# Centring h in place on GpSimd for the covariance, and moving copies on ScalarE, in a two-layer convolution kernel

## The chip, the core and the metric

The program runs on one core of a Trainium2 chip. The metric is the device time of one execution, in microseconds (us). The core's engines are TensorE (PE in the profile, its weight loads PEld), VectorE (DVE), ScalarE (ACT), GpSimd (POOL) and SyncE (SP), which issues most DMAs. Each engine works through its own list of instructions in order and waits on semaphores for the others.

## What is computed

Layer 0 makes position-dependent 7x7 filters from x and applies them. Layer 1 is a bottleneck block with batch normalisation over the batch; its second half is where the change lies. Cut to that:

```python
x = _L0_conv_ref(x, ...)                                  # (4, 256, 64, 64)
h = relu(_bn_train(_conv(x, w1, 1, 0), g1, b1))           # 64 channels
h = relu(_bn_train(_conv(h, w2, 1, 1), g2, b2))           # 64 channels, 3x3
h = _bn_train(_conv(h, w3, 1, 0), g3, b3)                 # 256 channels, 1x1
return relu(h + residual)                                 # residual is layer 1's x
```

`_bn_train` subtracts the mean of each channel over batch and pixels and divides by the root of its variance plus 1e-5.

## The kernel before

Most of the 822 us is layer 0 (to about 670 us). After it come the 3x3 convolution (680 to 740 us), whose result lies in `y`, eight images of 128 partitions x 1024 (two rows' halves of 64 channels share the partitions), then three short stages that this document is about.

**Batch norm 2 and ReLU (742 to 760 us).** VectorE works out `scale` and `shift` from statistics; ScalarE applies them with ReLU in place, image by image (`relu(i, ...)`, line 1274, semaphore `relu2`), and also sums each image. The first image goes in two halves.

**Covariance (745 to 767 us).** The variance after the last 1x1 convolution is not measured on its 256 channels. It is worked out from the 64x64 covariance of h and the weights. For that h is needed with pixels on the partitions, so 16 blocks of 512 columns go through a loop of three engines:

- `hT_of(k)` on TensorE transposes four 128-column tiles of block k (image k//2) into one of four PSUM banks, `hT_bank(k)`. Ahead of it `centre(k)` (line 1687) fills the bank with minus a per-channel constant c, the larger of 0 and batch norm 2's offset, and the transposes add to it.
- The block is split in a high part (fp32r) and a low part, the rest: a cast by VectorE (line 2181) or, for blocks 11, 13 and 15 (`UPPER_BY_ACT`), a copy by ScalarE (`upper(k)`), and then a subtraction by VectorE (`hT_parts`, line 1760). Both go to `hT[:, k % 2]`, so block k may be written once `gram(k-2)` is done.
- `gram(k)` (line 1712) multiplies the parts on TensorE. TensorE's list is transposes of k, product k-2, transposes of k+1, and so on; the first four blocks have no bank to wait for.

**Batch norm 3 (767 to 771.6 us).** A chain between VectorE and TensorE (`link` makes each operation wait for the one before) ends in `affine(2, 2, ...)`, which gives `scale` and `shift` of the last layer; ScalarE takes a root in between.

**Last layer (770 to 817 us).** The 1x1 convolution is 32 products m of 1024 columns (`last(m)`), each of two times three matmuls on the high and low parts of h (`h2_hi`, `h2_lo`; `h_hi` and `h_lo` in the profile) and of the weights. VectorE scales a product and adds the residual (line 2302, `f_added`), ScalarE adds `shift` and applies ReLU (line 1311, `f_out`), SP stores 1 MB after every second one (line 576). Product m waits for `f_added` of m-4, since there are four pairs of banks.

The parts of h come from two lists that fill gaps: ScalarE copies the high part of an image (`h2_high(i)`, line 957) right behind the ReLU of the next image, and GpSimd subtracts it from `y` (line 951, `h2_lo_done`). The outputs of unit 0 overwrite `y[:, 4:8]`, so ScalarE's first output waits for six low parts and its third for eight. A load of the residual into `y[:, 0:4]` waits for four.

Quoted, since the order within it matters:

```python
link(dve.tensor_tensor(gm[:, 10:12], gm[:, 4:8:2], gm[:, 4:8:2], ALU.mult))      # L2290
link(dve.tensor_tensor(mv[:, 12:12 + width], mv[:, 2:2 + width], gamma, ALU.mult))  # L2187
dve.tensor_tensor(scale[:, i:i + width], mv[:, 10:10 + width], gamma, ALU.mult)     # L2190
dve.scalar_tensor_tensor(out=shift[:, i + j:i + j + 1], in0=mv[:, 10 + j:11 + j], scalar=mv[:, 12 + j:13 + j],
                         in1=beta[:, j:j + 1], op0=ALU.mult, op1=ALU.add)           # L2192, twice
```

## Time and profile before

| | us |
|---|---|
| median of 3 runs (822.2 to 824.45) | 822.55 |
| the profiled execution | 823.44 |
| its span, first to last instruction | 821.6 |
| its granted TensorE clock, mean | 0.993 |

| engine | busy us (share of the span) |
|---|---|
| PE | 781.9 (95%) |
| DVE | 659.2 (80%) |
| ACT | 382.0 (46%) |
| POOL | 350.3 (43%) |

The span leaves out 1.8 us of the execution (823.44 less 821.6). Starts are counted from the span's first instruction. A row of a timeline joins neighbours of one form (x4), and "idle before" names what ended an engine's idle time. Shares over the whole span say little on the three short stages, which are read by themselves below.

### The profile page before, as it was taken

The numbers are of one execution on the slowest core, as the hardware profiler recorded it, in microseconds if no ns is written. First come the engines' busy times: TensorE is split into PE (matmuls) and PEld (weight loads), VectorE is DVE, ScalarE is ACT, GpSimd is POOL, SyncE is SP. The second block draws the span as 40 slices with busy tenths as digits, with TensorE's granted clock in tenths as the row PEclk, the third lists the DMA queues.
The fourth block names the chain that finished last, engine by engine and source line by source line (L and its number), as shares of the span: only waits on it lengthen the run. The fifth ranks groups of instructions, "written<-read, shape, count | busy, mean of one in ns | idle before, by whom it ended". The sixth has DMA issues, their size and how long they took to land.

```text
span 821.6 us, 13801 instructions
## 1 busy us (share of the span) xinstructions
PE 781.9 (95%) x4973; PEld 715.1 (87%) x4973; DVE 659.2 (80%) x908; ACT 382.0 (46%) x663; POOL 350.3 (43%) x253
## 2 busy tenths in 40 slices
PE   6799989999999999999999999999998998999996
PEld 2259988899999999999999999999997886777785
DVE  4989798897699588868977995888648676978896
ACT  3542222444344434434433434344326777727586
POOL 4345663484268238524852682385220012515300
PEclk9899999999999999999999999999999999999998
DMA  9932235957994899499588948885887869805598
GB/s 271 374 137 53 52 80 158 234 153 202 179 243 117 237 177 243 114 242 193 151 211 173 246 116 236 154 211 126 208 154 232 267 196 307 321 1 196 202 376 353
DMA packets 250108, 162.17 MB, mean 197 GB/s; under 512 B 191881, under 2 KB 232826, under 8 KB 247226
## 3 DMA queue, kind: packets, MB, share of 16 engines
q1 hardware_dynamic: 241322, 141.83, 66.4%
q10 hardware_dynamic: 8720, 19.47, 7.3%
q8 instruction: 41, 0.67, 0.4%
q14 instruction: 25, 0.20, 0.1%
HBM read 99.48 MB, written 56.36 MB: 190 GB/s over the span
## 4 chain that ended last, share of the span: by engine, by line
PE 78%; DVE 9%; issue 4%; DMA 3%; ACT 3%; POOL 1%; SPq 1%; DVEq 0%; ACTq 0%; POOLq 0%
PE ps L1319 21%; PE ps L1321 21%; PE ps L1320 21%; PE ps L1439 4%; PE ps L1455 3%; PE ps L1489 3%; DVE logit L1941 1%; DMA b2raw<-in_L_conv_b 1%; PE ps L1712 1%; DMA bands<-wide 1%; DVE whole L1851 1%; PE ps L1331 1%; DVE wpart L1801 1%; POOL ring L875 1%; PE ps L1704 1%
## 5 line engine op out<-in xcount | busy, mean ns | idle before, releaser
L875 POOL TENSOR_TENSOR ring<-whole,ring 128x576 fp32r<-128x576 f32 x112 | 194.9, 1746 | 281.3 <-ACT ring L957 281.3
L1319 PE MATMUL ps<-w_hi,ring 128*128 128x336 f32 x832 | 275.5, 331 | 6.7 <-POOL ring L875 3.8
L1321 PE MATMUL ps<-w_hi,ring 128*128 128x336 f32 x832 | 262.7, 316 | 0.0
L1320 PE MATMUL ps<-w_lo,ring 128*128 128x336 f32 x832 | 261.4, 314 | 0.0
L1319 PEld LDWEIGHTS ps<-w_hi,ring 128*128 128x128 f32 x832 | 157.3, 189 | 16.9 <-issue 10.6
L1320 PEld LDWEIGHTS ps<-w_lo,ring 128*128 128x128 f32 x832 | 157.3, 189 | 0.0
L1321 PEld LDWEIGHTS ps<-w_hi,ring 128*128 128x128 f32 x832 | 156.4, 188 | 0.0
L957 ACT ACTIVATE ring<-whole 128x576 fp32r<-128x576 f32 x112 | 87.1, 781 | 91.9 <-POOL whole L870 53.1
L957 ACT ACTIVATE band_hi<-ps 128x320 fp32r<-128x320 f32 (+1 forms) x128 | 53.1, 419 | 127.5 <-PE ps L1439 119.9
L1319 PE MATMUL ps<-band_hi,xT_hi 128*128 128x224 f32 (+2 forms) x320 | 94.6, 296 | 1.6 <-DVE xT_lo L1760 1.2
L1321 PE MATMUL ps<-band_hi,xT_lo 128*128 128x224 f32 (+2 forms) x320 | 92.3, 288 | 0.0
L1320 PE MATMUL ps<-band_lo,xT_hi 128*128 128x224 f32 (+2 forms) x320 | 92.3, 288 | 0.0
L1851 DVE SCALAR_TENSOR_TENSOR whole<-xbuf 128x576 f32<-128x576 f32 x80 | 81.0, 1018 | 8.5 <-POOL ring L875 8.3
L1760 DVE TENSOR_TENSOR band_lo<-ps,band_hi 128x320 fp32r<-128x320 f32 (+1 forms) x128 | 57.9, 457 | 24.9 <-ACT band_hi L957 24.0
L957 ACT ACTIVATE xT_hi<-ps 128x512 fp32r<-128x512 f32 x64 | 37.9, 596 | 74.1 <-PE ps L1455 72.3
L886 POOL TENSOR_TENSOR xbuf<-xbuf 128x1152 f32<-128x1152 f32 x24 | 65.2, 2719 | 0.9
L1319 PEld LDWEIGHTS ps<-band_hi,xT_hi 128*128 128x128 f32 x320 | 60.7, 190 | 3.8 <-issue 1.8
L1760 DVE TENSOR_TENSOR xT_lo<-ps,xT_hi 128x512 fp32r<-128x512 f32 x64 | 43.6, 684 | 25.1 <-ACT xT_hi L957 25.1
L1941 DVE SCALAR_TENSOR_TENSOR logit<-ps,logit 128x480 f32<-128x480 f32 x80 | 52.3, 653 | 13.5 <-PE ps L1321 9.6
L1439 PE MATMUL ps<-ident,raw 128*128 128x128 f32 x352 | 60.6, 276 | 2.1 <-DVE band_lo L1760 1.7
L1320 PEld LDWEIGHTS ps<-band_lo,xT_hi 128*128 128x128 f32 x320 | 60.7, 190 | 1.0
L1321 PEld LDWEIGHTS ps<-band_hi,xT_lo 128*128 128x128 f32 x320 | 60.9, 190 | 0.0
(228 smaller groups left out, 1353.5 us busy)
## 6 DMA issues: line engine op xcount, KB each, us to landing
xq<-in_x SPq DMA_DIRECT2D x108, 256.0 KB, 4.7
raw<-bands SPq DMA_DIRECT2D x32, 768.0 KB, 7.1
xbuf<-in_x SPq DMA_DIRECT2D x16, 1024.0 KB, 8.9
x_dram<-x ACTq DMA_DIRECT2D x31, 512.0 KB, 5.2
bands<-wide SPq DMA_DIRECT2D x64, 199.0 KB, 5.0
x1in<-x_dram SPq DMA_DIRECT2D x6, 2048.0 KB, 20.4
out<-x1in SPq DMA_DIRECT2D x12, 1024.0 KB, 3.9
bands<-wide SPq DMA_DIRECT2D x3, 1792.0 KB, 15.9
```

Of the source, the lines that this page charges most:

```text
L875: pool.tensor_tensor(split(k, 1), positions(whole[:, k % TBUFS, :], 0, 2), split(k, 0).bitcast(F32), ALU.subtract).then_inc(sig_lo_done, 1)
L886: pool.tensor_tensor(a, b, a, ALU.subtract).then_inc(c_done, 1)
L957: return act.activation(dst, src, ACT.Copy)
L1319: pe.matmul(dst, l_hi, r_hi_, start=first, stop=False, **kw)
L1320: pe.matmul(dst, l_hi, r_lo_, start=False, stop=False, **kw)
L1321: return pe.matmul(dst, l_lo, r_hi_, start=False, stop=last, **kw)
L1439: mm = pe.transpose(bank[:, i * P:(i + 1) * P], src, ident[:, :])
L1455: mm = pe.transpose(bank[:, t * C + kb * P:t * C + (kb + 1) * P], src[:, kb, 4 * t:4 * t + 4, g % 2::2], ident[:, :])
L1489: mm = pe.matmul(bank, v1pack[:, cb, :], r[:, cb, :], start=(cb == 0 and j == 0), stop=(cb == CB - 1 and j == 1))
L1760: return dve.tensor_tensor(dst, a, b, ALU.subtract)
L1851: dve.scalar_tensor_tensor(out=dst, in0=a, scalar=factor, in1=b, op0=ALU.mult, op1=ALU.add).then_inc(done, 1)
L1941: dve.scalar_tensor_tensor(out=dst, in0=m, scalar=factor, in1=src, op0=ALU.mult, op1=ALU.add).then_inc(comb_done, 1)
```

## The change

Instead of adding -c in PSUM by a product for each block, GpSimd subtracts c from h in place in `y` after the ReLU (nine `tensor_scalar`, one for each half of image 0 and one for each further image, semaphore `centred`). The transposes and the high parts wait for `centred` in place of `relu2`. The low parts stay on GpSimd, behind the nine. Since h is then centred in the last layer too, its mean and the covariance's mean are the same vector, and one column of the mean product goes. ScalarE takes the high parts of seven blocks instead of three, and its high parts of h stand behind them. Of the warming products after the 3x3 convolution there are 12 instead of 5.

```diff
-        UPPER_BY_ACT = (11, 13, 15)
+        UPPER_BY_ACT = (3, 5, 7, 9, 11, 13, 15)
...
             pool.memset(cov[:, :], 0.0).then_inc(cov_zero, 1)
-            pool.memset(one[:, :].bitcast(F32), 1.0).then_inc(one_made, 1)
...
+            pool.wait_ge(center_done, 3)
+            for i, c0, c1, made in [(0, 0, HALF, 1), (0, HALF, SPX, 2)] + [(i, 0, SPX, i + 2) for i in range(1, 8)]:
+                pool.wait_ge(relu2, made)
+                pool.tensor_scalar(y[:, i, c0:c1], y[:, i, c0:c1], gm[:, 2:3], None, ALU.add).then_inc(centred, 1)
             for i in range(8):
                 pool.wait_ge(h2_hi_done, i + 1)
...
             def h2_high(i):
-                act.wait_ge(relu2, i + 2)
+                act.wait_ge(centred, i + 2)
                 copy(h2_hi[:, i, :], y[:, i, :]).then_inc(h2_hi_done, 1)
...
             for i in range(1, 8):
                 relu(i, 0, SPX, i)
-                if i < 7:
-                    h2_high(i - 1)
-            upper(11)
-            h2_high(6)
+                if i >= 3:
+                    upper(2 * i - 3)
+            h2_high(0)
             upper(13)
-            h2_high(7)
+            h2_high(1)
             upper(15)
+            for i in range(2, 5):
+                h2_high(i)
             act.wait_ge(bn_dve, BN3_ROOT)
             root(mv[:, 8:10], gm[:, 12:14])
+            for i in range(5, 8):
+                h2_high(i)
...
-            for k in range(4):
-                centre(k)
-            warm(5)
+            warm(12)
...
                 if k >= 4:
                     pe.wait_ge(hT_lo_done, k - 3)
-                    centre(k)
-                pe.wait_ge(relu2, i + 2 if k else 1)
+                pe.wait_ge(centred, i + 2 if k else 1)
...
-            dve.tensor_scalar(center[:, :], ident[:, :], gm[:, 2:3], -1.0, ALU.mult, ALU.mult).then_inc(center_done, 1)
-            dve.wait_ge(center_done, 3)
-            dve.tensor_reduce(gm[:, 2:3], center[:, :].bitcast(F32), AX_X, ALU.add).then_inc(center_done, 1)
+            dve.tensor_scalar(gm[:, 2:3], gm[:, 2:3], -1.0, None, ALU.mult).then_inc(center_done, 1)
...
-            link(dve.tensor_scalar(gm[:, 1:2], gm[:, 3:4], 1.0 / (B * H * W), None, ALU.mult))
...
-            link(dve.tensor_copy(gm[:, 4:8], ps[:, 6, 0:4]))
-            link(dve.tensor_tensor(gm[:, 10:12], gm[:, 4:8:2], gm[:, 4:8:2], ALU.mult))
+            link(dve.tensor_copy(gm[:, 4:6], ps[:, 6, 0:2]))
+            link(dve.tensor_tensor(gm[:, 10:12], gm[:, 4:6], gm[:, 4:6], ALU.mult))
```

ScalarE's list from the ReLU of image 6 to the root, before; `hT<-ps` is a block's high part, `h_hi<-y` an image's:

```order
L1274 ACTIVATE y,sums<-y,shift,scale 128x1024
L957 ACTIVATE h_hi<-y 128x1024 [waits relu2]
L1274 ACTIVATE y,sums<-y,shift,scale 128x1024
L957 ACTIVATE hT<-ps 128x4x128 [waits gram_done,hT_ps]
L957 ACTIVATE h_hi<-y 128x1024 [waits relu2]
L957 ACTIVATE hT<-ps 128x4x128 [waits gram_done,hT_ps]
L957 ACTIVATE h_hi<-y 128x1024 [waits relu2]
L957 ACTIVATE hT<-ps 128x4x128 [waits gram_done,hT_ps]
L1188 ACTIVATE mv<-gm,sums 128x2 [waits bn_dve]
```

The same stretch now:

```order
L1275 ACTIVATE y,sums<-y,shift,scale 128x1024
L958 ACTIVATE hT<-ps 128x4x128 [waits gram_done,hT_ps]
L1275 ACTIVATE y,sums<-y,shift,scale 128x1024
L958 ACTIVATE hT<-ps 128x4x128 [waits gram_done,hT_ps]
L958 ACTIVATE h_hi<-y 128x1024 [waits centred]
L958 ACTIVATE hT<-ps 128x4x128 [waits gram_done,hT_ps]
L958 ACTIVATE h_hi<-y 128x1024 [waits centred]
L958 ACTIVATE hT<-ps 128x4x128 [waits gram_done,hT_ps]
L958 ACTIVATE h_hi<-y 128x1024 [waits centred] x3
L1189 ACTIVATE mv<-gm,sums 128x2 [waits bn_dve]
L958 ACTIVATE h_hi<-y 128x1024 [waits centred] x3
```

Before, six of eight high parts of h stood ahead of block 11's part; now all eight stand behind it, and three of them behind the root.

GpSimd's last instructions now; before, the eight `h_lo<-y,h_hi` came right behind the `step_lo` ones:

```order
L941 TENSOR_TENSOR step<-yin 128x1056 [waits step_lo_done,h1_hi_done,relu1]
L944 TENSOR_TENSOR step_lo<-step,step_hi 128x1056 [waits h1_hi_done]
L949 TENSOR_SCALAR y<-y,gm 128x512 [waits relu2,center_done]
L949 TENSOR_SCALAR y<-y,gm 128x512 [waits relu2]
L949 TENSOR_SCALAR y<-y,gm 128x1024 [waits relu2] x7
L952 TENSOR_TENSOR h_lo<-y,h_hi 128x1024 [waits h2_hi_done] x8
```

All eight low parts now stand behind the centring of the last image.

## Rows read from the trace of the kernel before

**Rows 1.** Busy time of each engine in a stretch (start:end, length, busy, clock, DMA):

```profile
740.00:760.00 20.00, 18.89 (x119) 15.07 (x117) 16.70 (x32) 15.99 (x24) 11.74 (x5) 1.00 0.54 201
```

**Rows 2.** Timeline of VectorE in the loop (start us, us, engine, line, operation, names, forms):

```profile
748.68 0.68 DVE L2181 CAST hT<-ps 128x512 fp32r<-128x512 f32 x1
749.40 0.69 DVE L1760 TENSOR_TENSOR hT<-ps,hT 128x512 fp32r<-128x512 f32 x1
750.01 0.68 DVE L2181 CAST hT<-ps 128x512 fp32r<-128x512 f32 x1
...
763.45 0.69 DVE L1760 TENSOR_TENSOR hT<-ps,hT 128x512 fp32r<-128x512 f32 x1 [0.44 <-ACT hT L957]
...
765.77 0.69 DVE L1760 TENSOR_TENSOR hT<-ps,hT 128x512 fp32r<-128x512 f32 x1 [0.30 <-ACT hT L957]
```

**Rows 3.** Timeline of TensorE, loop and first and last products of the last layer:

```profile
761.55 0.60 PE L1704 MATMUL ps<-ident,y 128*128 128x128 f32 x4
761.91 0.72 PE L1712 MATMUL ps<-hT 128*128 128x256 f32 x4
762.46 0.39 PE L1687 MATMUL ps<-center,one 128*128 128x512 f32 x1
...
770.88 0.39 PE L1319 MATMUL ps<-h_hi,v_hi 128*128 128x512 f32 x1
...
813.88 0.39 PE L1321 MATMUL ps<-h_hi,v_lo 128*128 128x512 f32 x1
```

**Rows 4.** Timeline of ScalarE, end of image 1's ReLU, block 11's high part, first outputs:

```profile
747.05 0.19 ACT L1274 ACTIVATION_READ_ACCUMULATOR y<-y,shift,scale 128x1 f32 x1
...
760.26 0.60 ACT L957 ACTIVATE hT<-ps 128x512 fp32r<-128x512 f32 x1
760.75 1.05 ACT L957 ACTIVATE h_hi<-y 128x1024 fp32r<-128x1024 f32 x1
...
773.00 4.83 ACT L1311 ACTIVATE y<-x1in,shift 128x1024 f32<-128x1024 f32 x4 [2.16 <-DVE x1in L2302]
```

**Rows 5.** Groups of GpSimd by form (count, busy us, mean ns, idle before):

```profile
L951 POOL TENSOR_TENSOR h_lo<-y,h_hi 128x1024 fp32r<-128x1024 f32 x8 | 18.9, 2408 | 23.6 <-ACT h_hi L957 23.6
...
L930 POOL MEMSET v_hi<- 128x1024 f32 x1 | 1.0, 960 | 47.8 <-PE ps L1439 47.8
...
L838 POOL TENSOR_SCALAR_AFFINE_SELECT gavg<-gavg 128x128 f32<-128x128 f32 x3 | 0.9, 294 | 0.4
```

**Rows 6.** Timeline of VectorE, then of GpSimd, in layer 0 around 262 us:

```profile
262.41 0.28 DVE L1978 TENSOR_TENSOR me<-smx,inside 128x112 f32<-128x112 f32 x1
262.72 2.77 DVE L1984 TENSOR_TENSOR wide<-probs,me 128x784 f32<-128x784 f32 x1
265.41 1.98 DVE L1851 SCALAR_TENSOR_TENSOR whole<-xbuf 128x576 f32<-128x576 f32 x1
...
260.22 4.43 POOL L886 TENSOR_TENSOR xbuf<-xbuf 128x1152 f32<-128x1152 f32 x2
264.61 2.15 POOL L875 TENSOR_TENSOR ring<-whole,ring 128x576 fp32r<-128x576 f32 x1
```

**Rows 7.** Forms of line 1978 on VectorE (count, ns min/median/max, first and last start):

```profile
L1978 DVE TENSOR_TENSOR me<-smx,inside x8: 274/276/2179, 125.7 to 625.6; 128x112 f32<-128x112 f32 x8
```

**Rows 8.** Timeline of GpSimd and of VectorE around batch norm 3:

```profile
748.26 18.85 POOL L951 TENSOR_TENSOR h_lo<-y,h_hi 128x1024 fp32r<-128x1024 f32 x8 [23.62 <-ACT h_hi L957]
...
769.81 0.16 DVE L2290 TENSOR_TENSOR gm<-gm 128x2 f32<-128x2 f32 x1
...
771.22 0.34 DVE L2192 SCALAR_TENSOR_TENSOR shift<-mv,bn 128x1 f32<-128x1 f32 x2
771.60 4.96 DVE L2302 SCALAR_TENSOR_TENSOR x1in<-ps,scale,x1in 128x1024 f32<-128x1024 f32 x4
```

**Rows 9.** Stretches after the last product (columns as Rows 1):

```profile
816.00:818.00 2.00, 0.00 (x0) 0.00 (x0) 0.00 (x0) 0.84 (x1) 0.00 (x0) 0.87 0.82 336
818.00:820.00 2.00, 0.00 (x0) 0.00 (x0) 0.00 (x0) 0.00 (x0) 0.00 (x0) 0.50 1.07 442
```

More of the change, by code:

```diff
@@ L267, in build @@
         quad = sb(h1s, "quad", [P, C])
-        center = sb(h1s, "center", [P, P], F32R)
-        one = sb(h1s, "one", [P, P], F32R)
-        rest = sb(h1s, "rest", [P, 2 * MID1 * 9 - 2 * C - 3 * P])
+        rest = sb(h1s, "rest", [P, 2 * MID1 * 9 - 2 * C - P])
         v3raw = sb(h1s, "v3raw", [P, CB, 2, MID1])
@@ L325, in build @@
         c2_done, c2_copied, c2_sum, c2_stat = sem("c2_done"), sem("c2_copied"), sem("c2_sum"), sem("c2_stat")
-        vT_done, center_done, cov_zero, one_made = sem("vT_done"), sem("center_done"), sem("cov_zero"), sem("one_made")
+        vT_done, center_done, cov_zero, centred = sem("vT_done"), sem("center_done"), sem("cov_zero"), sem("centred")
         h2_hi_done, upper_act = sem("h2_hi_done"), sem("upper_act")
@@ L2269, in _ @@
             dve.wait_ge(relu2, 9)
-            dve.wait_ge(center_done, 4)
+            dve.wait_ge(center_done, 3)
             link(dve.tensor_reduce(gm[:, 3:4], sums[:, 0:9], AX_X, ALU.add))
@@ L2288, in _ @@
             dve.wait_ge(means_ps, 1)
-            link(dve.tensor_copy(gm[:, 4:8], ps[:, 6, 0:4]))
-            link(dve.tensor_tensor(gm[:, 10:12], gm[:, 4:8:2], gm[:, 4:8:2], ALU.mult))
-            link(dve.tensor_scalar(mv[:, 2:4], gm[:, 5:8:2], -1.0, None, ALU.mult))
+            link(dve.tensor_copy(gm[:, 4:6], ps[:, 6, 0:2]))
+            link(dve.tensor_tensor(gm[:, 10:12], gm[:, 4:6], gm[:, 4:6], ALU.mult))
+            link(dve.tensor_scalar(mv[:, 2:4], gm[:, 4:6], -1.0, None, ALU.mult))
             dve.wait_ge(sums_ps, 1)
```

11 lines of the change are left out of this document (3 added, 8 removed).

## Prediction

> **What bounds the kernel now.** I read the engines' stretches first [rows 1]: in the 20 us that hold batch norm 2 and the covariance loop no engine is full, but TensorE (18.9) and VectorE (16.7) are near it, so the order of steps decides. VectorE's timeline [rows 2] shows why: a block costs a cast and a subtraction, 1.33 us from cast to cast (748.68 to 750.01), with no idle time before them, and the loop ends with the subtraction of block 15 at 766.46. TensorE's timeline [rows 3] shows 0.36 us for four transposes (761.55 to 761.91) and 0.55 for a product (761.91 to 762.46), and then one product after the other in the last layer: 31 of them from 770.88 to 814.27, 1.40 us each. That layer is bound by TensorE, and 7.3 us pass from its last product to the end of the span. So the change can act on two times: when the loop ends, and when VectorE may begin to empty the banks of the last layer (771.60, [rows 8]), since product 4 waits for the first emptying.
>
> **The loop, made shorter.** Twelve centring products go from it; they lay beside VectorE's work, which set the pace, and are worth nothing by themselves. Four of 13 casts on VectorE go, for ScalarE's copies of 0.60 us [rows 4]. A pair of blocks then costs VectorE at least 1.33 + 0.61 = 1.94 us. The wait that comes in its place is a chain over four blocks: subtraction 0.69, product of that block 0.55, transposes 0.36, next product until its end 0.72, ScalarE's copy 0.60, subtraction 0.61, cast 0.72 [rows 2, 3, 4], with 0.2 for handing over 4.45, or 2.23 a pair. The last pair of before took 2.32 (763.45 to 765.77, [rows 2]) with a centring product in it. I take 2.23, with 1.94 and 2.32 as its bounds.
>
> **The centring, added on GpSimd.** No row shows a `tensor_scalar` there. A memset of the same shape, which reads nothing, took 0.96 us, and the subtraction, which reads two operands, 2.41; a select of 128 columns with one operand took 0.294, or 2.35 if it grows with the columns [rows 5]. One operand is half way: 1.7, bounds 0.96 and 2.41. It is on the path once, in filling the loop: image 1's ReLU ends at 747.24 [rows 4], so its transposes begin at 749.1, the product of block 0 stands between, and the cast of block 2 begins at 749.1 + 0.36 + 0.72 + 0.1 = 750.3 where it was 748.68. Seven pairs later, 15.6 us, the loop ends at 765.9 instead of 766.46: 0.55 earlier. The Trainium skill (GPSIMD Engine Reference, Engine selection) calls GpSimd roughly at line rate with one input. No run here shows that; with some 1.1 us for the centring, an estimate from that page, everything below would come 0.6 us earlier.
>
> **The low parts, moved.** This is the term that counts. The first high part of h now stands behind block 11's, which is copied at 750.3 + 5 x 2.23 - 1.3 = 760.1 (five pairs on, less the copy and the subtraction); so the high part of image 0 is ready at 760.6 + 1.05 = 761.7, and GpSimd works from then for 8 x 2.36 = 18.9 us [rows 8], until 780.6. Before, it was done at 767.11, ahead of the last steps of batch norm 3. Now it runs through all of them, without a gap.
>
> What that does is told by [rows 6] and [rows 7]. `me<-smx,inside`, a sum of two operands in SBUF, takes 0.28 us, and once 2.18. At 262.72 line 1984, with two SBUF operands again, began while GpSimd's operation ran (260.22 for 4.43, two of them, to 264.65), and ended at 265.49: it stood still until GpSimd was through. GpSimd's next operation, in its queue since 264.61, ran then, to 266.76; and line 1851, which VectorE had issued at 265.41, before line 1984 was even done, waited it out, to 267.39. So such an operation waits for the end of the one that GpSimd is at, and GpSimd's next goes ahead of VectorE's next. Operations that read one operand from PSUM don't wait: the casts and subtractions of the loop keep their 0.69 us with GpSimd busy from 748.26 on [rows 2, 8].
>
> In batch norm 3 five operations of VectorE read two SBUF operands: L2290, L2187, L2190 and L2192 twice. They took 0.16 us or so because GpSimd had stopped [rows 8]. Now GpSimd's operations end at 761.7 + 2.36 k: 764.1, 766.4, 768.8, 771.1, 773.5, 775.9, 778.2, 780.6. L2290 comes up at 769.81 - 0.55 = 769.3 and is let through at 771.1, L2187 at 773.5, L2190 at 775.9, the two L2192 at 778.2 and 780.6. If another step (L2291) is caught too, the end stays, because GpSimd has nothing left after 780.6. VectorE begins at 780.8 instead of 771.60. The Trainium skill (SBUF — State Buffer, SBUF: two separate sides) says that such a pair takes the shared port as an exclusive lock for the whole instruction, and names no size below which it does not. No row here shows it for one or two columns, which is what these five have.
>
> **From there to the end.** TensorE has three products' lead over product 4, so what counts is product 4: before at 770.88 + 3 x 1.40 = 775.1, now at 780.8 + 1.24 [rows 8] = 782.1, 7.0 later. In between TensorE stands still for over 7 us. After its last product ended at 814.27 its granted clock was 0.87 in the mean from 816 to 818 and 0.50, the 1.2 GHz level, from 818 on [rows 9]. So it should come back at half clock. What that costs no row shows; at half clock a product takes up to 1.4 us more, so none to two and a half products' worth, 0 to 3.4 us; I take 1.7. ScalarE's first outputs wait for six and eight low parts (775.9, 780.6), which is earlier than VectorE now gives them anything, and the stores follow as before. The remaining edits cost nothing: one link of the chain less lies before the last product, the smaller mean product is off the path, the 12 warming products end before the first transposes, and the load into `y[:, 0:4]` comes at 771, with 34 us left.
>
> Sum: +7.0 + 1.7 = 8.7 us. The profiled execution would have a span of 821.6 + 8.7 = 830.3 and take 832.1; it lies 0.9 above the median of 822.55, from which I count: **831.2**. Bounds of the case: 829.4 (no fall of the clock) to 833.0.
>
> **Rivals.**
> 1. *Not slower: tiny operations are not held up.* If operations of one or two columns slip through, batch norm 3 ends 0.55 earlier. Then the outputs are what is late: ScalarE's third waits for the eighth low part, 780.6 instead of some 775.5, and 30 outputs at 1.21 or less ([rows 4], 4.83 for four, paced by VectorE) end at 816.9 or before, as now. The stores then come closer together than DMA moves them: 15 MB from 783 at 2.4 to 2.5 us each (442 GB/s in [rows 9] at the best) and 1.5 for the landing end at 820.5 to 822. So -1.0 to +0.5, say 822.2. For it: no row has so few columns. Against it: the rows with 112, 784 and 576 columns stand still alike, whatever their own work.
> 2. *Some are caught.* If the neighbours L2190 and L2192 pass together, VectorE begins at 776.1, product 4 at 777.4, +2.3: 824.9. If one boundary is saved, 778.5: +4.7 and little of the clock, 827.5.
> 3. *GpSimd's centring at 2.41 us.* Then it paces the loop, the last image is centred at 764.6, the low parts end at 783.5 and the whole comes to 834.
>
> **How the numbers follow.** The forecast 0.56, rival 1 0.18, rival 2 0.19 (0.06 at 825 and 0.13 above), rival 3 0.07. The forecast, rival 2 and the near side of rival 3 make up about 0.8: 824.0 to 833.2. A measurement of this kernel tells a change from none at about 0.3%, 2.5 us. Slower by more: 0.56 + 0.14 of rival 2 + 0.07 = 0.77. Within: 0.05 + 0.15 of rival 1 = 0.20. Faster, if pairs reach 1.94 us and nothing is held: 0.03.
>
> **What would show it.** In the profile of the changed kernel: L949's mean; VectorE's subtractions of odd blocks 2.2 us apart and the last one ending near 766; L2187, L2190 and L2192 (by their names `mv<-mv,bn`, `scale<-mv,bn`, `shift<-mv,bn`) at around 2.3 us each instead of 0.2, each ending just after one of GpSimd's low parts; `x1in<-ps,scale,x1in` beginning near 781; a gap of 7 us on TensorE and a granted clock of 0.5 after it. The forecast is wrong if these steps keep their 0.2 us while GpSimd is busy, or if GpSimd is done before 771.

## The result, and the profile after

The changed kernel takes **833.17 us** in the median (832.59 to 835.63, 4 runs), the kernel before 823.5 (822.2 to 825.26) beside it. The ratio is 1.0122, with a 95% interval of 1.0091 to 1.0152. The forecast was 831.2, in a range of 824.0 to 833.2. So the sign and most of the size came out. The working did not: one term was several microseconds too small, another several too large, and the end is set by a third thing. The profiled execution took 833.44, with a span of 831.6, 10.0 more than before.

GpSimd's timeline and its groups by form in the changed kernel (start, us; in the groups count, busy us, mean ns, idle before). They answer to [rows 5] and [rows 8].

```profile
744.83 23.00 POOL L949 TENSOR_SCALAR y<-y,gm 128x512 f32<-128x512 f32 x9 [20.72 <-ACT y L1275]
767.79 11.69 POOL L952 TENSOR_TENSOR h_lo<-y,h_hi 128x1024 fp32r<-128x1024 f32 x5
781.07 7.16 POOL L952 TENSOR_TENSOR h_lo<-y,h_hi 128x1024 fp32r<-128x1024 f32 x3 [1.58 <-ACT h_hi L958]
...
L949 POOL TENSOR_SCALAR y<-y,gm 128x1024 f32<-128x1024 f32 x7 | 19.8, 2848 | 0.1
L949 POOL TENSOR_SCALAR y<-y,gm 128x512 f32<-128x512 f32 x2 | 3.1, 1567 | 20.7 <-ACT y L1275 20.7
```

The centring takes 2.85 us for an image, not 1.7, more than the subtraction of two operands (2.38). GpSimd stands in it for 23 us without a gap, and the loop ends with it: the last three subtractions of VectorE's odd blocks begin at 765.15, 767.99 and 770.81, 2.8 us apart. The low parts begin at 767.79 and end at 788.23. In between GpSimd stands still once, for 1.58 us, for want of a high part.

VectorE from the last steps of batch norm 3 on, and ScalarE in the same stretch and at its first outputs (before: [rows 8] and [rows 4]):

```profile
775.20 0.16 DVE L2280 COPY gm<-ps 128x2 f32<-128x2 f32 x1
775.39 1.78 DVE L2281 TENSOR_TENSOR gm<-gm 128x2 f32<-128x2 f32 x1
777.20 2.31 DVE L2282 TENSOR_SCALAR mv<-gm 128x2 f32<-128x2 f32 x1
779.54 0.16 DVE L2284 TENSOR_TENSOR gm<-ps,gm 128x2 f32<-128x2 f32 x1
...
780.80 2.48 DVE L2293 SCALAR_TENSOR_TENSOR x1in<-ps,scale,x1in 128x1024 f32<-128x1024 f32 x2
...
779.74 0.30 ACT L1189 ACTIVATE mv<-gm,sums 128x2 f32<-128x2 f32 x1 [6.22 <-DVE gm L2284]
779.94 2.94 ACT L958 ACTIVATE h_hi<-y 128x1024 fp32r<-128x1024 f32 x3
783.65 2.38 ACT L1315 ACTIVATE y<-x1in,shift 128x1024 f32<-128x1024 f32 x2 [0.77 <-POOL h_lo L952]
788.26 2.34 ACT L1315 ACTIVATE y<-x1in,shift 128x1024 f32<-128x1024 f32 x2 [2.23 <-POOL h_lo L952]
```

Two operations are held up (lines 2281 and 2282), not five. The copy ahead of them reads PSUM and takes 0.16 us with GpSimd busy. Then comes the gap in GpSimd's row: the sixth high part stands on ScalarE behind the root (line 1189), and the root waits for line 2284. So GpSimd has nothing to do until batch norm 3 is nearly through, and VectorE's last five steps meet nobody. VectorE begins to empty the banks at 780.80, which is the prediction's time, for other reasons. ScalarE's third output then waits for the eighth low part until 788.26.

TensorE (first row: transposes waiting for GpSimd) and its stretches (start:end, length, PE busy, clock, DMA share, GB/s):

```profile
750.82 1.12 PE L1699 MATMUL ps<-ident,y 128*128 128x128 f32 x4 [2.17 <-POOL y L949]
...
749.00:756.00 7.00, 5.18 (x24) 0.51 0.24 96
760.00:773.00 13.00, 9.62 (x74) 1.00 0.01 1
773.00:780.00 7.00, 6.52 (x18) 0.51 0.23 74
...
790.00:820.00 30.00, 30.00 (x130) 1.00 0.97 400
```

The granted clock was at its half level, 1.2 GHz, twice, each time after TensorE had stood idle for part of the stretch before (it was busy for 2.3 of the 5 us from 744 to 749, and for 9.62 of the 13 from 760 to 773). From 790 on DMA is busy for 0.97 of the time at 400 GB/s. In the kernel before it still had room (0.91 and 378 GB/s from 780 to 800).

### The profile page after: what moved, and what is told of

Read it like the earlier page. It is cut to its first block, busy times and chain, and to the rows that moved or that the text cites. A ratio compares the mean times of both kernels' runs of the same rounds, so it can differ in the third digit from the quotient of the medians.

```text
span 831.6 us, 13805 instructions
## 1 busy us (share of the span) xinstructions
PE 784.7 (94%) x4964; PEld 719.3 (86%) x4964; DVE 658.2 (79%) x902; ACT 383.0 (46%) x667; POOL 370.2 (45%) x261
## 4 chain that ended last, share of the span: by engine, by line
PE 76%; DVE 10%; issue 4%; POOL 4%; ACT 3%; DMA 1%; SPq 0%; DVEq 0%; ACTq 0%; POOLq 0%
PE ps L1323 21%; PE ps L1325 21%; PE ps L1324 21%; PE ps L1443 4%; PE ps L1459 3%; PE ps L1493 3%; POOL y L949 2%; DVE whole L1845 1%; DVE logit L1935 1%; DMA b2raw<-in_L_conv_b 1%; DVE wsum L1795 1%; DVE wpart L1795 1%; POOL ring L873 1%; POOL whole L868 1%; ACT yin L1205 1%
## 5 line engine op out<-in xcount | busy, mean ns | idle before, releaser
L873 POOL TENSOR_TENSOR ring<-whole,ring 128x576 fp32r<-128x576 f32 x112 | 192.5, 1724 | 283.2 <-ACT ring L958 283.2
L958 ACT ACTIVATE ring<-whole 128x576 fp32r<-128x576 f32 x112 | 87.3, 783 | 92.3 <-POOL whole L868 49.9
L1845 DVE SCALAR_TENSOR_TENSOR whole<-xbuf 128x576 f32<-128x576 f32 x80 | 77.3, 972 | 8.5 <-POOL ring L873 8.2
```

Source lines behind the costliest of these rows:

```text
L873: pool.tensor_tensor(split(k, 1), positions(whole[:, k % TBUFS, :], 0, 2), split(k, 0).bitcast(F32), ALU.subtract).then_inc(sig_lo_done, 1)
L958: return act.activation(dst, src, ACT.Copy)
L1845: dve.scalar_tensor_tensor(out=dst, in0=a, scalar=factor, in1=b, op0=ALU.mult, op1=ALU.add).then_inc(done, 1)
```

## The experiments

The start of the first ReLU of this part moves between 743.2 and 746.3 from one profiled execution to another, whatever was changed behind it. So the table counts from it. The columns are the end of the loop's last subtraction, the start of VectorE's emptying of the banks of the last layer, the end of the last low part, the end of the span, and the last one less each of the two before it. "Ratio" is the time against the kernel before, with its 95% interval, where there were enough runs.

| kernel | loop | emptying | last low part | end | end - emptying | end - low part | ratio |
|---|---|---|---|---|---|---|---|
| before | 22.15 | 27.29 | 22.80 | 77.33 | 50.0 | 54.5 | 1 |
| changed | 27.77 | 37.06 | 44.49 | 87.89 | 50.8 | 43.4 | 1.0122 [1.0091, 1.0152] |
| e1 centring of one column | 21.10 | 29.73 | 37.12 | 80.26 | 50.5 | 43.1 | 1.0028 [1.0011, 1.0045] |
| e5 copies alone | 21.13 | 29.70 | 37.12 | 80.45 | 50.7 | 43.3 | 1.0028 [1.0011, 1.0045] |
| e6 centring alone | 27.62 | 44.02 | 42.52 | 92.43 | 48.4 | 49.9 | 1.0167 [1.0126, 1.0208] |
| e9 centring, two operands | 22.46 | 31.10 | 38.52 | 81.70 | 50.6 | 43.2 | 1.0046 [1.0032, 1.0061] |
| e3 GpSimd pauses | 27.74 | 32.89 | 44.81 | 86.62 | 53.7 | 41.8 | 1.0137 [1.0113, 1.0161] |
| e4 TensorE kept busy | 27.64 | 37.13 | 44.57 | 87.70 | 50.6 | 43.1 | 1.0128 [1.0100, 1.0156] |
| e2 highs before root | 27.76 | 44.23 | 42.73 | 92.04 | 47.8 | 49.3 | one run |
| e10 last two gated | 27.62 | 39.43 | 44.24 | 87.51 | 48.1 | 43.3 | one run |
| e11 last three gated | 27.64 | 37.14 | 44.35 | 86.14 | 49.0 | 41.8 | one run |
| e17 changed again | 27.73 | 37.03 | 44.47 | 86.3 | 49.3 | 41.9 | one run |
| e7 prices | 22.14 | 33.90 | 33.59 | 83.7 | 49.8 | 50.1 | one run |
| e8 two more copies | 23.14 | 28.29 | 23.30 | 78.60 | 50.3 | 55.3 | 1.0023 [1.0008, 1.0037] |
| e12 six copies | 23.19 | 28.34 | 25.12 | 78.18 | 49.8 | 53.1 | 1.0017 [1.0003, 1.0032] |

Three theories stood at the start. **Price**: the centring's 2.85 us make the loop and the low parts late. **Lock**: the held operations of batch norm 3 make product 4 late. **Clock**: TensorE at half clock does. One thing to keep in mind with single runs: the changed kernel's own two profiled executions (changed, e17) end 1.6 us apart.

### The two halves of the change, and the price

**e1** (line 949 of the changed kernel):

```diff
-pool.tensor_scalar(y[:, i, c0:c1], y[:, i, c0:c1], gm[:, 2:3], None, ALU.add)
+pool.tensor_scalar(y[:, i, c0:c0 + 1], y[:, i, c0:c0 + 1], gm[:, 2:3], None, ALU.add)
```

> The changed kernel, but GpSimd centres only one column of each block (the rest of the centring is left out, so the rows of h stay uncentred). What it asks: is it the centring's 2.85 us per 128x1024 block that makes the changed kernel late, or the low parts that still run through batch norm 3? Price theory: GpSimd stood in line from 744.8 to 767.8 for 22.8 us of centring and the loop's last product came 5.06 us later than before. With some 0.1 us a block instead, VectorE sets the pace (about 2.23 us a pair), the last product of the loop ends near 766 (772.31 in the changed kernel), and the low parts run from about 761 to 780 instead of 767.8 to 788.2. If no operation of VectorE is held up by them, VectorE begins to empty the banks near 771 and the span is back at 821 to 823 us. Lock theory: five operations of batch norm 3 with two SBUF operands, or with one, wait one after the other for the ends of low parts at about 771, 773.5, 776, 778.4, 780.7; VectorE begins at about 780.8 and the span is 828 to 830 us. Clock: TensorE stands still for some 7 us in batch norm 3 in the lock theory and 0.5 is seen after it.

**e5** (the kernel before with ScalarE's new list and `UPPER_BY_ACT = (3, 5, 7, 9, 11, 13, 15)`, centring products kept; `h2_high` waits for `relu2`):

> The kernel before with one half of the change: ScalarE's seven high parts of the transposes and its high parts of h2 later, but the centring products of TensorE stay and GpSimd does not centre. This is the half whose working stood in the prediction without the disputed price. Lock theory (the working of the prediction with a centring price of nought): the loop ends at about 765 to 766 us, the low parts run from about 760 to 779, VectorE begins to empty the banks at 779 to 781, span 828 to 830 us, 6 to 8 us over the kernel before. Price theory alone (only the centring costs): the loop ends earlier than before and nothing is late; span 820 to 822 us, the same as before or up to 1 us faster, or 1 us slower since the outputs of ScalarE wait for the last low part.

**e6** (the changed kernel with the list that ScalarE had before, and `UPPER_BY_ACT = (11, 13, 15)`):

> The kernel before with the other half: GpSimd centres h in place, no centring products, but ScalarE keeps three high parts of the transposes and its early high parts of h2. Price theory: GpSimd is again at centring from 744.8 to 767.8 without a gap, so the loop's last product ends at about 772.3, 5 us later than before, whoever does the copies; the low parts stand behind the last centring in GpSimd's queue and run without a gap from 767.8 to 786.7. The operations of batch norm 3 (from about 773) are each held until the end of one of these: five ends from 774.9 on are 774.9, 777.2, 779.6, 782.0, 784.3, so VectorE begins at about 784.5 and the span is 832 to 836 us. If only the two waits seen in the changed kernel occur, product 4 is at about 780 to 783 and the span is 829 to 832 us, set by DMA from the second store on.

Measured: 1.0028, 1.0028 and 1.0167. With the centring's length taken away, three quarters of the 1.2% are gone (e1). The rest is there with the copies alone (e5): they make the loop 1.0 us shorter and the kernel some 2 us slower. The centring alone costs more than the whole change, 1.7% (e6), so the two halves don't simply add up. Price and lock theory were each half right: e5 has no dear centring and is slower all the same, and it begins to empty the banks at 773.5, where the lock theory expected 779 to 781. In e5, GpSimd's and VectorE's timelines:

```profile
760.37 11.85 POOL L951 TENSOR_TENSOR h_lo<-y,h_hi 128x1024 fp32r<-128x1024 f32 x5 [36.26 <-ACT h_hi L957]
773.79 7.14 POOL L951 TENSOR_TENSOR h_lo<-y,h_hi 128x1024 fp32r<-128x1024 f32 x3 [1.58 <-ACT h_hi L957]
...
768.53 1.34 DVE L2293 TENSOR_TENSOR gm<-gm 128x2 f32<-128x2 f32 x1
769.91 2.33 DVE L2294 TENSOR_SCALAR mv<-gm 128x2 f32<-128x2 f32 x1
```

The holds (the time that a small operation of VectorE stands still beside a running one of GpSimd) are there without any centring, 1.34 and 2.33 us, and again there are two and then GpSimd's gap. e6 showed something that no theory had, for its high parts are all made before batch norm 3:

```profile
745.55 22.86 POOL L949 TENSOR_SCALAR y<-y,gm 128x512 f32<-128x512 f32 x9 [20.74 <-ACT y L1275]
768.38 18.61 POOL L952 TENSOR_TENSOR h_lo<-y,h_hi 128x1024 fp32r<-128x1024 f32 x8
...
775.96 11.04 DVE L2278 TENSOR_TENSOR gm<-gm 128x2 f32<-128x2 f32 x1
787.04 0.17 DVE L2279 TENSOR_SCALAR mv<-gm 128x2 f32<-128x2 f32 x1
...
788.48 3.67 DVE L2290 SCALAR_TENSOR_TENSOR x1in<-ps,scale,x1in 128x1024 f32<-128x1024 f32 x3
```

One operation on two columns stood for 11.04 us, over four ends of low parts, until GpSimd had ended its last. What the prediction had read from [rows 6], that each end of a GpSimd operation lets one of VectorE in, doesn't hold here. In e7 below it does.

**e7**, prices of GpSimd's operations, in the kernel before at the start of the loop, where GpSimd is idle (cut; each of these and three memsets at n = 64 and 512, written into `h2_lo`; `a`, `b`, `c` are three of its images, `to` is `a` again, and each operation waits for the one before):

```diff
+price(pool.tensor_scalar(to, a, gm[:, 2:3], None, ALU.add))
+price(pool.tensor_scalar(to, b, gm[:, 2:3], None, ALU.add))
+price(pool.tensor_scalar(to, a, 1.5, None, ALU.add))
+price(pool.tensor_copy(to, b))
+price(pool.tensor_tensor(to, b, c, ALU.subtract))
+price(pool.tensor_tensor(to, a, gm[:, 2:3].to_broadcast([P, n]), ALU.add))
```

> The kernel before with 18 further operations on GpSimd in its idle time at the start of the covariance loop, one after the other, each at 64 and at 512 columns of 128 partitions: memset (three), tensor_scalar with a scalar from SBUF in place and not in place, tensor_scalar with an immediate, tensor_copy, tensor_tensor, and tensor_tensor with the one scalar column broadcast as its second operand. They write what the low parts write later. What it asks: what is dear about the centring (1.57 us for 512 columns and 2.85 for 1024 in the changed kernel, against 2.38 for a subtraction of two operands over 1024). If it is the scalar read from SBUF: the immediate form takes 0.6 to 0.9 us at 512 columns and the other 1.5. If it is tensor_scalar as such: both 1.5. If it is writing where it reads: the form that is not in place takes less. The broadcast tensor_tensor should take 1.2, half of 2.4. Memset 0.5.

```profile
750.46 1.69 POOL L963 MEMSET h_lo<- 128x512 f32 x3
752.25 1.57 POOL L964 TENSOR_SCALAR h_lo<-h_lo,gm 128x512 fp32r<-128x512 f32 x1
753.91 1.56 POOL L965 TENSOR_SCALAR h_lo<-h_lo,gm 128x512 fp32r<-128x512 f32 x1
755.56 1.49 POOL L966 TENSOR_SCALAR h_lo<-h_lo 128x512 fp32r<-128x512 f32 x1
757.12 0.61 POOL L967 CAST h_lo<-h_lo 128x512 fp32r<-128x512 f32 x1
757.81 1.29 POOL L968 TENSOR_TENSOR h_lo<-h_lo 128x512 fp32r<-128x512 f32 x1
759.18 1.04 POOL L969 TENSOR_TENSOR h_lo<-h_lo,gm 128x512 fp32r<-128x512 f32 x1
```

It is tensor_scalar as such: neither the scalar from SBUF (1.57 against 1.49) nor writing in place (1.57 against 1.56) makes it dear. A cast costs 0.61, and the same sum written with a repeated second operand 1.04.

**e9** uses that last form in the changed kernel:

```diff
-pool.tensor_scalar(y[:, i, c0:c1], y[:, i, c0:c1], gm[:, 2:3], None, ALU.add)
+pool.tensor_tensor(y[:, i, c0:c1], y[:, i, c0:c1], gm[:, 2:3].to_broadcast([P, c1 - c0]), ALU.add)
```

> The changed kernel with the centring written as a sum of two operands, the second one the single column of gm repeated over the columns, instead of a tensor_scalar. In e7_prices that form took 1.04 us at 512 columns and 0.29 at 64, the tensor_scalar 1.56 and 0.45; over 1024 columns this extrapolates to 1.9 us instead of 2.85. Price theory: GpSimd's centring fits into the loop's pace again (1.9 against 2.3 us a pair), the loop ends at about 766 instead of 771.5, as the prediction had it with 1.7 us, and the span falls from 831.6 to that of e1_one_column (826.1) or up to 1 us above: 826 to 827.5. If something else of the changed order is what makes the loop late, the span stays above 830.

```profile
L949 POOL TENSOR_TENSOR y<-y,gm 128x1024 f32<-128x1024 f32 x7 | 13.2, 1893 | 1.7 <-ACT y L1275 1.7
...
769.29 1.64 DVE L2281 TENSOR_TENSOR gm<-gm 128x2 f32<-128x2 f32 x1
770.97 2.33 DVE L2282 TENSOR_SCALAR mv<-gm 128x2 f32<-128x2 f32 x1
...
774.57 19.72 DVE L2293 SCALAR_TENSOR_TENSOR x1in<-ps,scale,x1in 128x1024 f32<-128x1024 f32 x16
```

1.893 us an image where 1.9 was expected. GpSimd now waits for ScalarE's ReLUs, the loop is 5.3 us shorter, the span 6.4 shorter, and the ratio falls from 1.0122 to 1.0046. That shows the price theory. It is also the forecast's own case, with a price near the one that it had assumed, and 1.0046 times 822.55 is 826.3, 4.9 below the forecast.

### What sets the end

**e3** lets GpSimd's fourth low part wait for the end of batch norm 3:

```diff
             for i in range(8):
+                if i == 3:
+                    pool.wait_ge(bn_dve, BN3_END)
                 pool.wait_ge(h2_hi_done, i + 1)
```

> The changed kernel with GpSimd's fourth low part behind the end of batch norm 3: nothing of GpSimd runs while VectorE computes batch norm 3. The two held operations (1.78 and 2.31 us in the changed kernel) then take some 0.16 us each, and VectorE begins to empty the banks at about 777 instead of 780.8. The low parts run from 777 and end at about 788.8, 0.6 later. Lock theory (the end follows from product 4): span 3.7 us shorter, 828. DMA theory (the end follows from ScalarE's outputs, which wait for the last low part, and from the stores behind them at 1 MB in about 2.4 us): span the same or up to 1 us longer, 831.5 to 832.5.

```profile
776.17 0.16 DVE L2283 TENSOR_TENSOR gm<-gm 128x2 f32<-128x2 f32 x1
776.36 0.17 DVE L2284 TENSOR_SCALAR mv<-gm 128x2 f32<-128x2 f32 x1
...
777.96 4.96 DVE L2295 SCALAR_TENSOR_TENSOR x1in<-ps,scale,x1in 128x1024 f32<-128x1024 f32 x4
```

The holds are gone (0.16 and 0.17 us), so GpSimd's running low parts are their cause. VectorE begins 4.2 us earlier, counted from the ReLU, and the time does not move (1.0137 against 1.0122, intervals overlapping). So in the changed kernel neither the holds nor the clock, which was 1.00 from 774 to 782 here, costs anything at the end.

**e4** gives TensorE more products of no use: `warm(18)` for `warm(12)`, `warm(3)` and `warm(10)` behind the transposes of blocks 0 and 1, `warm(2)` after blocks 7, 9, 11 and 13.

> The changed kernel with more of TensorE's warming products, which compute nothing that is used: 18 instead of 12 ahead of the loop, three and ten behind the transposes of blocks 0 and 1, and two after each of blocks 7, 9, 11 and 13, where TensorE waits for GpSimd's centring. In the changed kernel the granted clock was 0.5 from 749.2 to 756.0 and from 773.1 to 779.9. Clock theory: the second fall costs about 2.9 us of the way from the loop's last product to product 4 (5.6 and 5.1 us where the kernel before has 3.6 and 4.2); without it VectorE's held operations meet GpSimd's low parts in other places, but TensorE has its four products ready by 781, product 4 follows VectorE at 780.8 + 1.2, about 782, 1 us earlier. DMA theory (the end follows from the last low part, the second store and DMA): span unchanged within 0.5 us of 831.6 even with the clock at 1.00 throughout.

```profile
749.00:756.00 7.00, 6.13 (x42) 1.00 0.33 134
760.00:773.00 13.00, 10.78 (x80) 1.00 0.00 1
773.00:780.00 7.00, 6.19 (x22) 0.60 0.12 35
```

The clock stays at 1.00 through the loop, and the loop is as long as before (27.64 against 27.77): the first fall costs nothing, since TensorE waits for GpSimd anyway. The second fall stayed, so e4 says nothing of it. e3 does, and e1 and e9: both have 1.00 from 766 to 776 and end 43.1 and 43.2 us after the last low part, as the changed kernel does (43.4).

The table's two differences show what does set the end. Where the emptying begins before the low parts are through, the end comes 43.1 to 43.4 us after the last low part, or 41.8 to 41.9 (e3, e11, e17). e3 and e10 show it from both sides: their emptying begins 4.2 us earlier and 2.4 us later than the changed kernel's, their last low part ends within 0.3 us of its, and their ends, 86.62 and 87.51, lie within what the changed kernel's two executions have (86.3 and 87.89). Where the emptying begins after the low parts (e2, e6, and e13 to e16 below), the end comes 47.8 to 48.9 after the start of the emptying; with the low parts long done, TensorE's last layer makes it 50. The path of the first kind is last low part, ScalarE's third output, second store, and then 15 stores of 1 MB on a full DMA. ScalarE's last outputs, in the changed kernel and in e5, show that it is DMA that is behind there:

```profile
823.75 1.21 ACT L1315 ACTIVATE y<-x1in,shift 128x1024 f32<-128x1024 f32 x1 [0.18 <-DVE x1in L2293]
```

```profile
815.62 1.21 ACT L1314 ACTIVATE y<-x1in,shift 128x1024 f32<-128x1024 f32 x1 [0.18 <-DVE x1in L2305]
```

They end at 824.96 and 816.83, 6.6 and 7.5 us ahead of the end of the span; in the kernel before it was 4.8. e5's outputs end when those of the kernel before do, and its span is 2.7 us longer. That is the end rule of rival 1. What makes it 41.8 in some executions is open.

TensorE is close behind, though. In the changed kernel it has no idle time from 776.5 on. Product 4 begins at 783.02, after the first emptying has ended at 782.08, so it did not wait for VectorE: it came late since the loop had ended late and the first products ran at half clock. In e3, with the clock at 1.00, product 4 begins 2.9 us earlier, counted from the ReLU, and ScalarE's last output ends 2.0 us earlier (79.18 against 81.21); the stores behind the low parts hide it. An estimate from these numbers: with the 4.8 us that the kernel before takes from its last output to the end, TensorE's path alone would end the changed kernel at 86.0, 0.3 to 1.9 us before its two measured ends.

### When VectorE gets in

**e2** puts all of `h2_high(2)` to `h2_high(7)` ahead of the root in the changed kernel, so that low parts are ready all the time.

> The changed kernel with all of ScalarE's high parts of h2 ahead of the root of batch norm 3, so that GpSimd has a low part ready at every moment from 767.8 to 786.6 (in the changed kernel it stood still for 1.6 us from 779.5, for want of the sixth high part behind the root). Stream or idle rule: VectorE's product of gm (about 775.4) now stands still until the last low part begins or ends (784.2 or 786.6), batch norm 3 ends at about 786 to 788 instead of 780.8, and the span is 5 to 7 us longer than the changed kernel's 831.6. First-boundary rule: VectorE gets in at each end of a low part, with five or six operations held, 784 to 786.6, span 834 to 837. If what bounds the changed kernel is only the low parts through DMA: 1.6 us earlier, span 830.

Measured 840.39 us: the product of gm stood for 11.62 us (777.38 to 789.00) and got in only when GpSimd had stopped. Work that is ready earlier made the kernel slower: counted from the ReLU, it ends 4.2 us after the changed kernel and 5.7 after e17. (The rest of the difference in time lies ahead of the part that was changed.)

**e10** and **e11** gate low parts in e6, `if i == 6:` and `if i == 5:` with `pool.wait_ge(bn_dve, BN3_END)`.

> The kernel e6_centring_alone, in which GpSimd had eight low parts ready one behind the other and VectorE's first operation with two SBUF operands (776.0) stood for 11.0 us, over five ends of low parts, until the last had ended (787.0). Here GpSimd lets the last two low parts wait for the end of batch norm 3, so that the run of low parts that are ready ends with the sixth, at about 782.4. First-boundary rule (of the prediction): the operation gets in at the end of the low part that is running, 777.7, and the next one at 780.0. Stream rule: it gets in when the last ready low part begins (780.0) and the one-operand operation behind it when that ends (782.4); in the changed kernel and in the two other runs the first got in just as the fifth low part began, behind which none was ready. Idle rule: only when GpSimd stands still, 782.4. By the stream or the idle rule VectorE begins to empty the banks at 783.7, 4.8 earlier than in e6_centring_alone (788.5), and the last two low parts end at about 788.5; by the first-boundary rule it is the same 783.7 or a little earlier.

> As e10_last_two_gated, but already the sixth low part waits for the end of batch norm 3: only one low part is ready behind the one that runs when VectorE's operation with two SBUF operands comes up (about 775). In the changed kernel, in e1_one_column and in e5_copies_alone one was ready behind it too, and the operation got in between the two (after 1.3 to 1.8 us), while with two, four and four ready (e10, e6, e2) it stood until all had ended. If the number that is ready decides: it gets in between the two, at about 776.7, and the tensor_scalar behind it is held until the second has ended, 779.1. If the stream always has to end: the first is held until 779.1 and the second is not held. Either way VectorE begins to empty the banks at about 780.5, 2.4 earlier than in e10_last_two_gated.

Measured 832.82 and 833.27 us (e6: 838.31). The rows of e10, then of e11:

```profile
774.97 6.44 DVE L2280 TENSOR_TENSOR gm<-gm 128x2 f32<-128x2 f32 x1
```

```profile
776.68 4.13 DVE L2280 TENSOR_TENSOR gm<-gm 128x2 f32<-128x2 f32 x1
```

In both, VectorE got in when GpSimd came to the gate and stopped (781.40 and 780.80), and not between two low parts, as the idle rule has it (the tensor_scalar behind it then took 0.17 us). But in the changed kernel, e1, e5 and e9 it had got in between the fourth and the fifth. There it had come up 0.61 to 1.04 us into the fourth, e6, e10 and e11 at 0.61 or 0.62. So the moment was moved, with copies of two columns ahead of the product of gm in e6 (six here, and 1, 3 and 11):

```diff
+            for n in range(6):
+                dve.tensor_copy(gm[:, 4:6], ps[:, 6, 0:2]).then_inc(spare, 1)
+                dve.wait_ge(spare, n + 1)
             link(dve.tensor_copy(gm[:, 4:6], ps[:, 6, 0:2]))
```

> e6_centring_alone with one more copy of two columns from PSUM (0.19 us) on VectorE ahead of the product of gm, which there came up 0.61 us into the fourth low part and stood for 11.04 us, over five ends. Now it comes up at 0.80. Arrival rule (later than about 0.61 into the running low part gets in at its end): about 1.6 us, and the tensor_scalar behind it is then held in its turn. Queue rule (with several low parts ready it stays out to the end of the stream): about 10.9 us.

> As e13_later_by_1, with three more copies: the product of gm comes up 1.2 us into the fourth low part. Arrival rule: held for about 1.2 us, then in. Queue rule: about 10.5 us, to the end of the eighth low part.

> As e13_later_by_1, with six more copies: the product of gm comes up 1.75 us into the fourth low part. Arrival rule: held for about 0.6 us, then in. Queue rule: about 9.9 us.

> As e13_later_by_1, with eleven more copies: the product of gm comes up early again in a low part, 0.3 to 0.5 us into the fifth. Arrival rule: not let in at the next end, and, if nothing changes while it waits, held to the end of the eighth low part, about 9 us. Queue rule: the same. So this run tells the rules apart only together with the other three: with them let in and this one held, the moment of arrival decides.

It came up 0.77, 1.19, 1.80 and 2.22 us into the fourth low part (the eleven copies were not enough to reach the fifth) and was held for 10.91, 10.49, 9.88 and 9.44 us, each time to the end of the eighth: in these four runs the moment decides nothing. Two last runs, the changed kernel again and e11 with two such copies:

> The changed kernel once more, nothing else: another execution. If the moment of arrival (0.61 us into the fourth low part) decides alone, the product of gm is let in at the end of the fourth low part again, as in the first profile (1.78 us), unless it comes up some hundredths of a microsecond earlier. If it differs from execution to execution, it may also stand to the end of the fifth, 4.1 us.

> e11_last_three_gated with two more small copies on VectorE ahead of the product of gm, which stood there from 0.61 us into the fourth low part to the end of the fifth (4.13 us). Now it comes up at 1.0 us. If the moment decides with one low part behind (0.61 to 1.04 us got in): it gets in after 1.4 us and the tensor_scalar is held 2.3. If the gate that follows decides (here a wait for VectorE, in the changed kernel a wait for ScalarE): 3.7 us and no hold for the tensor_scalar.

1.80 and 2.31 us in e17, at 0.59 into the low part: the changed kernel does the same in another execution. 3.74 us in e18, and no hold of the tensor_scalar. So what comes next in GpSimd's list may matter, but it isn't shown. With a gate that waits for VectorE behind the fifth low part, VectorE stays out until GpSimd has come to it (e11, e18). With a low part behind it that waits for ScalarE's high part, VectorE gets in one end earlier in five executions (changed, e17, e1, e5, e9), but not in e4, which has the same list (held for 4.17 us, from 0.55 into the fourth). For the time it made no difference: the tensor_scalar is then held in its turn, and the emptying begins at 37.03 to 37.14 in the changed kernel, e17, e4, e11 and e18 alike.

One trace goes against a rule of the stream altogether. In e7 the added operations made GpSimd late, so that all eight low parts, ready one behind the other, ran through batch norm 3, as the prediction had it:

```profile
760.31 18.75 POOL L972 TENSOR_TENSOR h_lo<-y,h_hi 128x1024 fp32r<-128x1024 f32 x8
...
770.97 1.10 DVE L2311 TENSOR_TENSOR gm<-gm 128x2 f32<-128x2 f32 x1
772.10 2.34 DVE L2312 TENSOR_SCALAR mv<-gm 128x2 f32<-128x2 f32 x1
...
774.67 2.11 DVE L2208 TENSOR_TENSOR mv<-mv,bn 128x2 f32<-128x2 f32 x1
777.02 2.06 DVE L2211 TENSOR_TENSOR scale<-mv,bn 128x2 f32<-128x2 f32 x1
779.37 2.47 DVE L2323 SCALAR_TENSOR_TENSOR x1in<-ps,scale,x1in 128x1024 f32<-128x1024 f32 x2
...
780.71 0.51 PE L1340 MATMUL ps<-h_hi,v_hi 128*128 128x512 f32 x1 [4.33 <-DVE x1in L2323]
```

Here four operations are held, and each gets in at the end of the low part that it had met: the product of gm came up 1.29 us into the fifth, with three more ready behind it, and was in at that one's end. So with two or more low parts ready behind the running one, VectorE stood to the end of the stream in seven executions (e2, e6, e10, e13 to e16) and got in at the next end in one (e7). What decides it is open.

### Is there a faster version?

**e8**: the kernel before with `UPPER_BY_ACT = (5, 9, 11, 13, 15)`, the two new copies behind the ReLUs of images 4 and 6.

> The kernel before, with ScalarE taking two more of VectorE's high parts in the covariance loop (blocks 5 and 9) and nothing else moved: the high parts of h2 stay early, so that the low parts still end at about 767, ahead of batch norm 3. In the run with seven copies the loop's last product ended 1.5 us earlier than before, but the low parts, 13 us later, held VectorE up and made the stores late. If that account is right, two more copies give 0.6 us each less ScalarE's wait for its turn: the loop ends 0.7 to 1.2 us earlier and the span is 820.5 to 821 instead of 821.6. If ScalarE is the bound of the loop (a ReLU, a high part and a copy are 2.8 us for a pair of blocks that takes 2.3), its ReLUs come late and the loop ends later than before: 822 to 823.

**e12**: blocks 5, 7, 9, 11, 13, 15, and GpSimd makes the high parts of images 0 and 4 itself:

```diff
+                if i in (0, 4):
+                    pool.wait_ge(relu2, i + 2)
+                    pool.tensor_copy(h2_hi[:, i, :], y[:, i, :]).then_inc(h2_hi_pool, 1)
...
```

> The kernel before, changed otherwise: ScalarE takes six high parts of the transposes (blocks 5, 7, 9, 11, 13, 15), and GpSimd makes two of ScalarE's high parts of h2 (of images 0 and 4) itself, which by the copy of e7_prices (0.61 us at 512 columns) cost it about 1.2 us each, ahead of its low parts of the same images. So ScalarE is not overloaded as in e8_two_more_copies, where VectorE waited 1.62 us for the copy of block 5, and the low parts still end at about 767.5, before batch norm 3. If so, the loop ends 1 to 1.5 us earlier than before, batch norm 3 is not held up, and the span is 820.3 to 821. If the low parts run into batch norm 3, one operation is held until they end, and the span is 821.5 to 823.

Both are slower by 0.2%: the loop is 1.0 us longer than before, not shorter. One row of VectorE in e8, one in e12, and the price of the cast in e12:

```profile
753.55 0.69 DVE L1762 TENSOR_TENSOR hT<-ps,hT 128x512 fp32r<-128x512 f32 x1 [1.62 <-ACT hT L957]
...
765.00 0.69 DVE L1766 TENSOR_TENSOR hT<-ps,hT 128x512 fp32r<-128x512 f32 x1 [1.59 <-ACT hT L962]
...
L952 POOL CAST h_hi<-y 128x1024 fp32r<-128x1024 f32 x2 | 2.1, 1040 | 21.4 <-ACT y L1279 21.4
```

A single copy that comes late on ScalarE, which has a ReLU, a high part and a copy for each pair, costs VectorE 1.6 us, more than two copies save. No run here beats the kernel before.

## Why the prediction was wrong, though its total came near

- **What bounds, a step that failed.** It named the loop's end and the start of the emptying. For the end of the last low part its sum had nothing, since it took the low parts to be through (780.6) before the emptying (780.8). They ended 7.4 us after its start (788.23 and 780.80), and that set the end. Only rival 1 had this path.
- **The loop.** 2.23 us a pair was taken, 2.32 was the upper bound; without dear centring it is 2.32 (VectorE's subtractions in e1: 761.60, 763.91, 766.23). From the ReLU that gave 21.6, and e1 and e5 have 21.1, e9 has 22.5. This step was right to 1 us.
- **The centring, the step that failed first.** The price was put at 1.7 us, between a memset and a subtraction, by the number of operands read, and both bounds were taken for safe. 2.85 us lies outside. No row of a tensor_scalar was there, so the upper bound needed a reason that it did not have. The place was right: with 2.41, rival 3 has GpSimd pacing the loop, which is what happened. Its total, 834, lies 0.8 from the measured one, but it rests on the same five holds.
- **The low parts.** Forecast from 761.7 to 780.6, found from 767.79 to 788.23. With the price that was assumed (e9) they run from 761.50 to 781.99. What is missing there is the 1.6 us gap.
- **Five held operations, the step that failed second.** Operations of two columns are held: right, shown by e3 and e5, and rival 1's premise falls. But there were two. The diff shows why: `h2_high(5)` stands behind `root`, which waits for batch norm 3, so the sixth low part can't run through it. The prediction called the stream gapless. And one of the two was a tensor_scalar with one operand in SBUF (line 2291 of the kernel before), which it had only named as possible. In e9, with nearly the assumed price, VectorE begins at 774.57 instead of 780.8.
- **The Trainium skill's lock** (SBUF — State Buffer, SBUF: two separate sides): it is exclusive and names no size, and the trace agrees down to two columns. What the prediction added from [rows 6], one entry at each end, held in e7, four times in a row, and in the five executions with two holds (changed, e17, e1, e5, e9). It was wrong in the ten others, in e6 by 9.3 us (787.0 instead of 777.7).
- **The Trainium skill's line rate** (GPSIMD Engine Reference, Engine selection): the 1.1 us for one input that the prediction estimated from it holds for the cast, 1.04 us, and not for the tensor_scalar, 2.85.
- **Product 4 and the clock, 1.7 us.** The 7 us for which TensorE was to stand still did not come: the loop ended late, the first products ran at half clock (6.52 of 7 us busy from 773 to 780), and product 4 did not wait for the emptying. What the half clock cost there, 2.9 us at product 4, stayed hidden behind the stores (e3).
- **Where its conditions held.** e7 had the gapless low parts, over before the emptying. There product 4 waits for the first emptying (780.66, product 4 at 780.71, after 4.33 us of idle time) and comes 4.5 us later than before, counted from the ReLU (35.24 against 30.76); TensorE's last product ends 6.15 later (76.11 against 69.96), so the half clock cost 1.7; the end comes 6.4 later. These steps of the forecast are right as mechanisms. In the changed kernel they did not apply.
- **The sum.** 7.0 + 1.7 against 10.0. The forecast's 780.8 was reached with a loop that ended 5.6 us later than forecast (771.50 against 765.9) and 5.6 us less from there to the emptying (9.3 against 14.9), and the end then came from elsewhere. Rival 1's end rule with the true low parts, 15 MB at 2.4 to 2.5 us and 1.5 from 790.6 on, gives 828.1 to 829.6, 2 to 3.5 short of the span. In times: the forecast's working was 4.9 us too high for its own case (e9), and the price that it missed took 6.3 (1.22% less 0.46% of 822.55). The total came near by luck, by errors that cancelled.

## To carry to other kernels

Price an operation that the trace doesn't show by its own form, not by its operand count, and where that can't be had, look for the same result in a form with a known price: here the same sum, written otherwise, took 1.89 us instead of 2.85 and gave back three fifths of the loss. Work moved out of a loop does not vanish; ask which later stage it now runs through, which engine's operations stand still beside it there, and whether its own inputs stand behind that stage. Where VectorE had to get past a stream of GpSimd's operations, a gap in the stream was worth more than having the stream's inputs ready earlier. And test a rule on every trace, also on those made for another purpose: that a ready stream keeps VectorE out to its end is contradicted here only by the trace of the price list.

## What was not expected of the hardware

- On GpSimd a tensor_scalar over 128x512 of f32 took 1.49 to 1.57 us with either kind of scalar, more than a tensor_tensor (1.29, and 1.04 with a repeated column) and 2.5 times a cast (0.61).
- A VectorE operation on two columns, SBUF to SBUF, stood for up to 11.6 us while GpSimd had ready operations one behind the other, over four ends. In seven of eight executions with two or more ready behind the running one it stood until GpSimd stopped; in the eighth (e7) it got in at the next end. A tensor_scalar with one SBUF operand is held as well (2.31 us).
